# Expert layers: chunks of the next layer's keys and values at other places, and the first tiles' rows ahead of the last key stores

## What is computed

```python
k = key @ Wk + bk          # per layer, key = value = ctx_1024
v = value @ Wv + bv
```

```python
gate_probs = softmax(x @ gate_w.T); expert_idx = argmax(gate_probs)
for e in range(8):
    ye = relu(x @ w1[e] + b1[e]) @ w2[e] + b2[e]
    out = out + where(expert_idx == e, ye * expert_w, 0)
```

## Time and profile before

| | |
|---|---|
| median of 3 runs | 4187.69 us (4187.18 to 4191.48) |
| the profiled execution's own time | 4189.45 us |
| its span in the profile | 4188.3 us |
| TensorE busy | 3591.2 us, 86% of the span |
| VectorE busy | 2198.8 us, 53% |
| ScalarE busy | 2085.0 us, 50% |
| GpSimd busy | 605.4 us, 14% |
| DMA moved | 422.70 MB, mean 101 GB/s |

### The profile page before, as it was taken

How to read it: one execution, slowest core, us unless ns; L and a number is a source line. 1 busy time by engine, 2 the same in 40 slices (tenths; PEclk the granted TensorE clock), 3 DMA queues, 4 the chain that set the end, 5 groups by cost and what they waited for, 6 DMA issues and landing times.

```text
span 4188.3 us, 54007 instructions
## 1 busy us (share of the span) xinstructions
PE 3591.2 (86%) x19494; PEld 1925.4 (46%) x19494; DVE 2198.8 (53%) x3456; ACT 2085.0 (50%) x4574; POOL 605.4 (14%) x617
## 2 busy tenths in 40 slices
PE   5999999978489999997894899999979788794993
PEld 2334343345223333325783233333259555583993
DVE  6766767737577777754004877777430211342332
ACT  2566666643156566673332466666723222352661
POOL 1112121001160620003011101100010100003013
PEclk7999999999689999997997899999989899996996
DMA  8132313035742522107648312211075500303556
GB/s 180 47 84 69 84 62 80 1 107 176 193 120 60 140 51 53 32 1 225 205 159 202 100 33 77 58 40 32 1 244 173 180 32 32 112 1 127 187 179 100
DMA packets 280002, 422.70 MB, mean 101 GB/s; under 512 B 52555, under 2 KB 206739, under 8 KB 277563
## 3 DMA queue, kind: packets, MB, share of 16 engines
q1 hardware_dynamic: 235238, 287.01, 25.4%
q0 software_dynamic: 27360, 98.58, 7.8%
q10 hardware_dynamic: 17141, 33.66, 2.3%
HBM read 281.09 MB, written 133.63 MB: 99 GB/s over the span
## 4 chain that ended last, share of the span: by engine, by line
PE 67%; DVE 16%; DMA 6%; issue 3%; POOL 3%; ACT 3%; SPq 1%; ACTq 0%; DVEq 0%; POOLq 0%
PE pv L1209 13%; PE m L1173 10%; DVE mxp L1060 10%; PE s L1195 9%; PE h L2130 8%; PE y L2139 8%; PE s L1464 2%; PE m L1230 2%; PE s L1147 2%; PE y L1481 2%; DMA xn<-ys,slot_u 1%; PE m L1222 1%; PE h L291 1%; SPq L94 1%; POOL xs L1925 1%
## 5 line engine op out<-in xcount | busy, mean ns | idle before, releaser
L1060 DVE TENSOR_REDUCE mxp<-m 128x1 f32<-128x802 f32 x1536 | 1446.2, 988 | 482.0 <-PE m L1173 479.8
L1296 ACT ACTIVATE e_t<-s 128x512 f32<-128x512 f32 (+1 forms) x2496 | 1357.4, 599 | 685.4 <-PE s L1195 684.5
L1173 PE MATMUL m<-kaug,qaug 97*128 97x401 bf16 x3072 | 809.9, 346 | 112.0 <-DMA qaug<-qready 46.3
L1195 PE MATMUL s<-qaug,kaug 100*128 100x512 bf16 (+1 forms) x2496 | 862.7, 384 | 14.7 <-ACT e_t L1296 11.8
L1209 PE MATMUL pv<-e_t,v 128*32 128x512 f32 (+1 forms) x4992 | 669.6, 608 | 0.2
L1195 PEld LDWEIGHTS s<-qaug,kaug 100*128 100x128 bf16 (+1 forms) x2496 | 235.4, 100 | 685.7 <-ACT e_t L1296 484.6
L1173 PEld LDWEIGHTS m<-kaug,qaug 97*128 97x128 bf16 x3072 | 274.5, 99 | 513.4 <-DVE mxp L1060 223.6
L2139 PE MATMUL y<-w,hT 128*128 (+1 forms) x1504 | 345.1, 383 | 11.7 <-DVE hT L1978 11.7
L2130 PE MATMUL h<-xtT,w 128*128 128x128 f32 x2496 | 297.8, 279 | 8.7 <-DMA w<-in_L_w 5.3
L2139 PEld LDWEIGHTS y<-w,hT 128*128 128x128 f32 x1504 | 282.0, 192 | 48.4 <-issue 6.4
L2130 PEld LDWEIGHTS h<-xtT,w 128*128 128x128 f32 x2496 | 291.2, 195 | 9.8 <-issue 9.2
(11 more groups left out here) (287 smaller groups left out, 3414.5 us busy)
## 6 DMA issues: line engine op xcount, KB each, us to landing
w<-in_L_w POOLq DMA_DIRECT2D x78, 1024.0 KB, 5.4
w<-in_L_w SPq DMA_DIRECT2D x24, 1024.0 KB, 13.4
kaug<-kparts SPq DMA_DIRECT2D x16, 1200.8 KB
kaug<-kready SPq DMA_DIRECT2D x32, 600.4 KB
kaug<-kready SPq DMA_DIRECT2D x16, 1200.8 KB
p_ctx<-in_ctxT SPq DMA_DIRECT2D x36, 512.0 KB, 5.8
values<-p_vb ACTq DMA_DIRECT2D x36, 512.0 KB, 5.3
kready<-p_ks SPq DMA_DIRECT2D x36, 384.0 KB, 6.2
```

The source lines that it names most:

```text
L1060: dve.tensor_reduce(a.mxp[:, u.g % 2, half, n:n + 1], a.m_slot[u.m % 2][:].rearrange("p (a n) -> p a n", a=2)[:, :, 0:PIECE + 1], AX.XY, A ...
L1173: m = pe.matmul(slot[:, 512 * k:512 * k + PIECE + 1], a.qaug[0:R_MAX, u.g, j, P * qc:P * qc + P], a.kaug[0:R_MAX, u.g, j, k0:k0 + PIECE + ...
L1195: pe.matmul(slot[0:KW[u.k], :], a.kaug[0:R_ALL, u.g, u.j, P * u.k:P * u.k + KW[u.k]], a.qaug[0:R_ALL, u.g, u.j, :], start=True, stop=True) ...
L1296: act.activation(a.e_t[0:KW[u.k], e % 2, u.j, :], a.s_slot[u.s % 3][0:KW[u.k], :], ACT.Exp).then_inc(s_free.sem, 1)
```

## The change

- The plan has five parts now: c0 and c1, c2 alone, c3 to c7, c8 to c13, c14 and c15. c2 stands between the logits and the ranks. c3 to c7 stand behind the ranks, c8 to c13 behind the last expert tile and in front of the norm, c14 and c15 in the tail.
- SyncE issues part 0's loads and stores in the middle of the eight loads of `w2`, and not behind them.
- Of c3 to c7 the last four key pieces (c6 and c7) are held: SyncE waits for the scatter, loads the first two tiles of rows, and only then loads the contexts of c9 and c10 and stores the held pieces, ahead of the loads of tiles 2 and 3.
- VectorE splits a piece behind three of four added tiles (`if q % 4`).
- Layers 0 and 3 have the same instructions as before.

```diff
+def prepare_sp(kn, p, part, leave=0):
+    held, chunks = [], p.parts[part]
+    for c in chunks:
+        if not leave or c["i"] + leave // DC <= chunks[-1]["i"]:
+            prepare_load_sp(kn, p, min(c["i"] + 4, len(p.chunks)))
         if c["b"] in p.in_parts:
             for x in c["keys"]:
                 held.append(x)
-                if len(held) > 2:
-                    store(held.pop(0))
+                if len(held) > max(2, leave):
+                    prepare_store_sp(kn, p, held.pop(0))
+    if leave:
+        return held
...
+def prepare_held_sp(kn, p, part, held):
+    prepare_load_sp(kn, p, min(p.parts[part][-1]["i"] + 4, len(p.chunks)))
+    for x in held:
+        prepare_store_sp(kn, p, x)
...
-                           ((2, ("pool",)), (5, ("dve",)), (5, ("dve",)), (4, ("dve",))))
+                           ((2, ("pool",)), (1, ("dve",)), (5, ("dve",)), (6, ("dve",)), (2, ("dve",))))
...
     for e in range(NE):
+        if a.p and e == NE // 2:
+            prepare_sp(kn, a.p, 0)
         sp.dma_start(a.w2[:, e, :, :], w["w2"][e].rearrange("(f p) n -> p f n", p=P)).then_inc(ld_w.sem, DMA)
...
     if a.p:
-        prepare_sp(kn, a.p, 0)
         prepare_sp(kn, a.p, 1)
+        held = prepare_sp(kn, a.p, 2, 4)
     sp.wait_ge(scatter.sem, scatter.at(a.K * NT))
...
-    for m in range(4):
+    for m in range(2):
+        load(m)
+    if a.p:
+        prepare_held_sp(kn, a.p, 2, held)
+    for m in range(2, 4):
         load(m)
...
-            if q % 2:
+            if q % 4:
                 prepare_split(kn, a.p, left[0:1], dve, "dve")
...
         m.then_inc(lg_full.sem, 1)
+    if a.p:
+        prepare_pe(kn, a.p, 1)
     pe.wait_ge(oh_made.sem, oh_made.at(1))
```

More of the change, by code:

```diff
@@ L252, in prepare_load_sp, with prepare_store_sp @@
         p.loaded += 1
-def prepare_sp(kn, p, part):
-    sp = kn.nc.sync
-    def store(x):
-        split, kept = kn.sema("p_split_" + x["by"]), kn.sema(f"p_k{x['k'] % p.RING}", DMA)
-        sp.wait_ge(split.sem, split.at(x["n"] + 1))
-        c0, n = x["c0"], x["cols"]
-        store_parts(sp, "k", kn.dram["kready"][x["b"], P * x["j"]:P * x["j"] + P, :, c0:c0 + n],
-                    p.ks[:, x["k"] % p.RING, :, 0:n], kept.sem)
-    held = []
-    for c in p.parts[part]:
-        prepare_load_sp(kn, p, min(c["i"] + 4, len(p.chunks)))
+def prepare_store_sp(kn, p, x):
+    split, kept = kn.sema("p_split_" + x["by"]), kn.sema(f"p_k{x['k'] % p.RING}", DMA)
+    kn.nc.sync.wait_ge(split.sem, split.at(x["n"] + 1))
+    c0, n = x["c0"], x["cols"]
+    store_parts(kn.nc.sync, "k", kn.dram["kready"][x["b"], P * x["j"]:P * x["j"] + P, :, c0:c0 + n],
+                p.ks[:, x["k"] % p.RING, :, 0:n], kept.sem)
+def prepare_sp(kn, p, part, leave=0):
[3 more added lines that the diff above has]
+            prepare_load_sp(kn, p, min(c["i"] + 4, len(p.chunks)))
         if c["b"] in p.in_parts:
@@ L271, in prepare_sp @@
                 held.append(x)
-                if len(held) > 2:
-                    store(held.pop(0))
+                if len(held) > max(2, leave):
+                    prepare_store_sp(kn, p, held.pop(0))
+    if leave:
+        return held
     for x in held:
-        store(x)
+        prepare_store_sp(kn, p, x)
+def prepare_held_sp(kn, p, part, held):
+    prepare_load_sp(kn, p, min(p.parts[part][-1]["i"] + 4, len(p.chunks)))
+    for x in held:
+        prepare_store_sp(kn, p, x)
 def prepare_pe(kn, p, part):
@@ L1884, in experts_sp @@
     a.dmas["scatter"] = a.K * NT
+    held = []
     if a.p:
-        prepare_sp(kn, a.p, 0)
         prepare_sp(kn, a.p, 1)
+        held = prepare_sp(kn, a.p, 2, 4)
     sp.wait_ge(scatter.sem, scatter.at(a.K * NT))
@@ L1907, in experts_sp @@
     if a.p:
-        prepare_sp(kn, a.p, 2)
         prepare_sp(kn, a.p, 3)
+        prepare_sp(kn, a.p, 4)
 def experts_pool(kn, a):
@@ L2077, in experts_dve @@
     if a.p and a.p.in_parts:
-        prepare_split(kn, a.p, a.p.keys_of(1), dve, "dve")
-        left = a.p.keys_of(2)
+        for part in (1, 2):
+            prepare_split(kn, a.p, a.p.keys_of(part), dve, "dve")
+        left = a.p.keys_of(3)
     for m in range(a.M + 1):
@@ L2159, in experts_pe @@
     if a.p:
-        prepare_pe(kn, a.p, 1)
+        prepare_pe(kn, a.p, 2)
         p_free = kn.sema("p_free")
-        pe.wait_ge(p_free.sem, p_free.at(a.p.ended(1)))
+        pe.wait_ge(p_free.sem, p_free.at(a.p.ended(2)))
     pe.wait_ge(ld_w.sem, ld_w.at(NE))
@@ L2185, in experts_pe @@
     if a.p:
-        prepare_pe(kn, a.p, 2)
+        prepare_pe(kn, a.p, 3)
         pe.wait_ge(t_free.sem, t_free.at(a.M))
@@ L2226, in experts_act @@
         prepare_act(kn, a.p, 1)
+        prepare_act(kn, a.p, 2)
     act.wait_ge(routed.sem, routed.at(1))
@@ L2241, in experts_act @@
     if a.p:
-        prepare_act(kn, a.p, 2)
+        prepare_act(kn, a.p, 3)
         norm_act(kn, "c", a.slots)
-        prepare_act(kn, a.p, 3)
+        prepare_act(kn, a.p, 4)
 def first_x_sp(kn, a, k):
```

4 lines of the change are left out of this document (2 added, 2 removed).

## The result

The change made the kernel slower: 4199.81 us (median of 11 runs, 4192.65 to 4208.89) against 4187.18 (4180.63 to 4194.28, 11 runs), ratio 1.0032, 95% interval 1.0023 to 1.0041. Forecast were 4168.0 us, a range of 4154 to 4184, and 0.79 for faster. The profiled execution of after took 4208.89 us (span 4207.7) and is the slowest of its eleven, 9 us above their median; before's took 4189.45.

What follows compares the result with a forecast made beforehand. TensorE, busy 86% of the span, was taken to bound the kernel. Terms of -2.7, -10.2 and -6.8 us sum to -19.7 on 4189.45, giving 4169.8; the median, 1.8 lower, gives 4168.0 us, range 4154 to 4184.

Steps and rivals of the forecast that it cites:

- Term 1: Between logits and ranks, both layers: c2 only partly fits a 3.73 us hole, so ranks come 5.5 us later.
- Term 2: Start of layer 1's experts: with SyncE's stores held, TensorE starts 2.7 us earlier, counted as -2.7 us.
- I cost that at nothing, narrowly: Layer 1's third tile: rows land by 2020, TensorE wants them at 2020.9, so no cost.
- a hole at tile 2: Layer 1's experts: a hole opening there, or a wait for rows over 10 us, would show Term 2 wrong.
- Term 3: Layer 1 before and behind the norm: norm later, but tail and stores shorter, -10.2 us in sum.
- I take 6 us later: Layer 1's norm: 6.9 us more of VectorE's splits make the transposes 6 us later.
- by the same ring: Layer 1 before the norm: TensorE's six chunks, slowed by the key buffers, fit ahead of transposes at 2236.4.
- The sign named for it: Layer 1 before the norm: ScalarE's waits for stores exceeding 30 us would show Term 3 wrong.
- Term 4: Layer 2: tail 13.8 us shorter, less 5.5 for late ranks and 1.5 for context loads, -6.8 us in sum.
- the transposes stay where they are: Layer 2's norm: 13.8 us of added chunks, less 1.9, fit the 12.24 us hole, so no delay.
- The ring paces the stretch before the norm: Rival, layer 1: chunks at 13.96 us each make transposes about 27 us late; +11.9 us, 4199.6 us; chance 0.07.

Runs made afterwards that it cites:

- groups A and D: Two of five sets of follow-up runs, each set made on one chip together with the kernel before; A and D had different chips.
- e4: Kernel before with only SyncE's new order in layer 1, the old chunk table in both layers: ratio 0.9999 to the kernel before.
- e7: The change with four tiles' rows instead of two ahead of the held stores, in both layers: ratio 0.9983 to the kernel before.
- e16: The kernel of e7 run once more on another chip: ratio 1.0023 to the kernel before.
- e1: The changed kernel run once more, for a second profile: ratio 1.0027 to the kernel before.
- e6: Kernel before with seven chunks in front of the norm and two behind it, in both layers: ratio 0.9986 to the kernel before.
- e5: Kernel before with only c2 put between the logits and the ranks, in both layers: ratio 1.0004 to the kernel before.
- e8: Kernel before, with part 0's stores amid the second weights and four tiles' rows ahead of the held stores in layer 1: ratio 0.9979.
- e10: Layer 1 as in e8; layer 2 as before but with seven chunks in front of the norm and two behind: ratio 0.9980 to the kernel before.

## Why the prediction was wrong

**Term 1 was right in its delay.** c2 behind the logits took 8.9 us in layer 1 and 9.7 in layer 2, its first eight matmuls 5.61 and 6.35 us where a chunk at full clock has 3.60: the granted clock was 0.50 in the last 4 us of the logits, as the earlier trace rows had it. The ranks came 6.6 and 6.4 us later for 5.5, of which 1.6 and 0.6 are longer logits. Whether they are passed on "in full" in layer 2 depends on the trace. Between before and after the first scatter is 5.8 later against the logits (28.1 for 22.3) and the first weights only 2.4 (50.8 for 48.4), since the wait for the scatter's landing fell from 6.06 to 2.67 us. In groups A and D that wait was short with the old table, too, and the weights came 3.7 to 5.7 us later for ranks 4.6 to 6.3 later. The experts' first tile comes 4.8 later in after, since the weights took 9.8 us to come instead of 7.4; for the contexts beside them 1.5 was taken.

**Term 2 failed twice, and both times at the price of stores in SyncE's queue.** The forecast's times are to be read against the logits, which begin 3.3 us earlier in after. c4 then ended as forecast (48.5 us behind their start for 48.4), c5 2.4 us late, c6 3.3 late. The eighteen stores of k 6 to 11 were given 16.5 us (1986.5 to 2003) and took 23.30, so that the first rows were issued at 72.8 for 65.4, c7's evictions, which wait for the same stores, came as much later, and TensorE started at 82.9 for 76.2: 6.7 us late, 4.0 later than before and not 2.7 sooner. The second failure is "I cost that at nothing, narrowly". The third tile's rows were to be issued 12.1 us behind the first tile's, and were 16.6 behind; in e4 it was 21.6 (1980.2 to 2001.8). They then needed 8.1 us to arrive, where the forecast had 4.4 for them and 8.8 for the first tile's rows in the same paragraph. The twelve stores between took 12.11 us in after, and 18.44 in e4, where all are of 512 columns; twelve of 512 columns had taken 17.78 before, 1.5 us each, so the price was in front of the author. Term: +12.0 at the third tile and +14.6 at the experts' end, for -2.7; within groups A and D +7.7 and +10.1 at the third tile and +9.7 and +12.9 at the end. e7 and e16 show the hole's part: without it the third tile comes at 85.5 and 86.1 instead of 90.1 to 98.3. At the experts' end little of that is left, 256.9 in both for 254.8 to 263.8, since TensorE then stands 6.06 and 5.39 us in front of the third tile's up matmuls. The sign that was named, a hole at tile 2, is the one that appeared.

**Term 3 failed at "I take 6 us later".** The stretch to the norm grew by 19.8 us in after, 12.6 in e1 against e4 (57.2 for 44.6). The prediction priced VectorE's 6.9 us more of splits and let TensorE's six chunks fit in front of the norm "by the same ring". They did not: before, the five chunks took 36.6 us for 24.5 unhindered (three full at 6.9, two small at 1.9), and the six of after 57.0 for 36.4. The ring's loop held TensorE up by 20.6 us instead of 12.1, and the norm's statistics stood behind the last splits. e6 shows the step by itself, without c2 and without the new order: 64.8 us with seven chunks for 43.6 with five (e5), and no gain in layer 1. The sign named for it did not appear: ScalarE's waits for stores were 20.1 us, below the 30 named and hardly above the 18.6 of before. The tail was 14.5 shorter for the 16.2 reckoned (6 + 10.2). The term's sum is +5.3 for -10.2.

**Term 4 failed at "the transposes stay where they are".** TensorE did what was reckoned only where its count reached the others in time: the norm 36.1 us behind the experts in e7 and 37.8 in e6, for 36.4 before and 35.8 in e5, and layer 2 shorter by some 17 and 16. Where it was late, the norm came at 44.8 to 47.1 and layer 2 gave nothing: -0.5 in after, 246.4 and 248.6 for 247.7 and 244.5 with the old table in group A, 247.3 and 248.6 for 243.9 in group D. The hole of 12.24 us in the earlier trace rows was no idle time to be filled at will; where the count is late, a stall of some us lies in its place.

**The rival that came true** is the slower one, "The ring paces the stretch before the norm", 4199.6 against a median of 4199.8. That is in good part luck. Its chunks were too slow (65.7 us for 57.0; its 36.8 for six unhindered chunks is 36.4 by its own 6.9 and 1.9), its "from about 13 us per chunk" was met by c10 and c12 only, and it knew neither the third tile's hole nor the late count; these made up for it. It had 0.07, on the argument that `q % 4` moves the first full split forward. c8 and c9 did then go at 6.9 us each; c10 and c12, further on, paid 12.7 and 18.6.

**Better than both kernels** is e8: the table of before, part 0's stores amid the second weights, four tiles' rows ahead of the held stores. 0.9979 and 0.9976 on two chips, once without and once with the late count, 9 to 10 us faster than before. Joined with the seven chunks in front of layer 2's norm (e10) it has 0.9980, no better, on a chip where the count is late. What it would be elsewhere was not tried.

## What to carry to other kernels

Price every entry of an in-order queue by the row that the trace has for it, also the entries in front of what is wanted second and third: rows for the first two tiles alone moved a hole of 16 us to the third, and four tiles' rows closed some 8 us of it for good. Compare the times of two traces only from a common event on, here the start of the logits, and not from the start of the span. A chunk moved into idle time is free only if its own resources (here four ring buffers and the stores that free them) pass at TensorE's pace there. And a hole can hide a stall that stands in the trace of another chip only: a gain that rests on filling it should be seen on more than one.
